# Twelve heads of the first attention batch scored inside the last convolution outputs, and one projection moved a batch later

## The reference, cut to what matters

```
h = silu(conv(x @ w_in_x)) * D * silu(x @ w_in_gate);  x = layernorm(x + h @ w_out)      # (8, 256, 512)
q = x @ Wq.T;  k, v = split(ctx @ Wkv_expand.T)                                          # 16 heads of 32
scores = where(causal, q @ k.T / sqrt(32), lowest);  attn = softmax(scores)
x = layernorm(x + (attn @ v) @ Wout.T)
x = layernorm(x + mixture_of_experts(x))
```

## Time and profile before

| What | us |
|---|---|
| median of 3 runs | 1043.26 |
| lowest and highest of them | 1036.83 and 1044.63 |
| the profiled execution | 1038.53 |
| its span, first to last instruction | 1036.7 |
| PE busy | 973.8 (94%) |
| DVE busy | 678.1 (65%) |
| ACT busy | 528.8 (51%) |
| POOL busy | 257.5 (25%) |

### The profile page before, as it was taken

The page is one execution under the profiler, slowest core; times in us unless marked ns, Lnnn a source line. Parts: engine busy times, 40 slices in busy tenths (PEclk is TensorE's granted clock), DMA queues, the critical chain, the costliest instruction groups (busy, mean ns, idle before and its releaser), DMA issues. The chain is left out here.

```text
span 1036.7 us, 17387 instructions
## 1 busy us (share of the span) xinstructions
PE 973.8 (94%) x5776; PEld 830.6 (80%) x5776; DVE 678.1 (65%) x1554; ACT 528.8 (51%) x1264; POOL 257.5 (25%) x373
## 2 busy tenths in 40 slices
PE   7899999999978999998889979999999999999996
PEld 6688888888867888887667769989888988778785
DVE  4737636378358788887567656777777775254576
ACT  5533414325358889889753146656656664221120
POOL 4610020102133333333530022222222220503040
PEclk9999999999996999998899999999999999999999
DMA  4503005021695989997540268778877882615041
GB/s 163 203 1 122 0 14 199 0 82 61 199 207 140 277 226 260 249 246 192 204 153 21 94 213 282 246 235 279 275 252 249 265 270 78 226 39 202 1 171 73
DMA packets 87758, 172.74 MB, mean 167 GB/s; under 512 B 8624, under 2 KB 36528, under 8 KB 85904
## 3 DMA queue, kind: packets, MB, share of 16 engines
q1 hardware_dynamic: 80560, 149.95, 46.5%
q0 software_dynamic: 7136, 22.03, 6.5%
HBM read 131.05 MB, written 37.49 MB: 163 GB/s over the span
## 5 line engine op out<-in xcount | busy, mean ns | idle before, releaser
L45 PE MATMUL a_ps_proj<-region_a_rounded,arena 128*128 128x512 f32 x272 | 107.8, 396 | 10.3 <-DVE region_a_rounded L369 6.2
L805 ACT ACTIVATE b_dump<-b_dump,b_peak 128x128 f32<-128x128 f32 (+1 forms) x256 | 113.2, 446 | 6.1 <-DVE b_peak L939 5.8
L45 PE MATMUL e_ps_h<-e_x_lo,e_gu_hi 128*128 128x256 f32 (+1 forms) x384 | 110.5, 288 | 2.6 <-DVE e_x_lo L2160 1.3
L47 PE MATMUL e_ps_h<-e_x_hi,e_gu_hi 128*128 128x256 f32 (+1 forms) x384 | 107.6, 280 | 0.0
L46 PE MATMUL e_ps_h<-e_x_hi,e_gu_lo 128*128 128x256 f32 (+1 forms) x384 | 107.5, 280 | 0.0
L46 PE MATMUL a_ps_proj<-region_a_rounded,arena 128*128 128x512 f32 x272 | 106.8, 393 | 0.0
L47 PE MATMUL a_ps_proj<-region_a_rounded,arena 128*128 128x512 f32 x272 | 106.8, 393 | 0.0
L388 DVE SCALAR_TENSOR_TENSOR f_region_b<-a_ps_proj,a_taps,f_region_b 128x510 f32<-128x510 f32 (+2 forms) x96 | 71.7, 746 | 40.8 <-ACT f_region_b L328 38.5
L939 DVE CUSTOM_DVE_ANT_0 b_dump<-b_ps_s,b_mask 128x128 f32<-128x128 f32 (+1 forms) x256 | 80.1, 352 | 22.4 <-PE b_ps_s L1140 19.4
L2166 DVE TENSOR_TENSOR e_gu_lo<-f_region_a,e_gu_hi 128x704 fp32r<-128x704 f32 x92 | 81.3, 887 | 14.9 <-ACT e_gu_hi L2072 14.2
L2072 ACT ACTIVATE e_gu_hi<-f_region_a 128x704 fp32r<-128x704 f32 x92 | 71.8, 784 | 23.1 <-PEq L1476 15.2
(11 more groups left out here) (407 smaller groups left out, 2662.1 us busy)
## 6 DMA issues: line engine op xcount, KB each, us to landing
f_region_a<-we_gate_up SPq DMA_DIRECT2D x88, 352.0 KB, 4.9
qk_split<-arena SPq DMA_DIRECT2D x24, 512.0 KB, 6.2
y_slots<-f_region_b SPq DMA_DIRECT2D x16, 512.0 KB, 4.0
f_x_next<-x SPq DMA_DIRECT2D x6, 1024.0 KB, 7.5
b_sk<-qk_split SPq DMA_DIRECT2D x24, 256.0 KB, 4.4
b_sq<-qk_split SPq DMA_DIRECT2D x24, 256.0 KB, 6.1
f_region_a<-we_down SPq DMA_DIRECT2D x12, 512.0 KB, 4.5
f_region_b<-we_down SPq DMA_DIRECT2D x11, 512.0 KB, 4.1
```

Of the source, the lines that this page charges most:

```text
L45: pe.matmul(out, a_hi, b_lo, start=first, stop=False)
L47: return pe.matmul(out, a_hi, b_hi, start=False, stop=last)
L805: ins = act.activation(dump[:, n % DUMPS, cols], dump[:, n % DUMPS, cols], ACT.Exp, scale=-1.0, bias=peak[:, u, k, i:i + 1], accum_out=tot ...
```

## The change

Four things, in one diff. First, the scores, maxima and totals of heads 0 to 11 of batch 0 move into the convolution's last group: after each `three_pass` of j = 5, 6 and 7 stands one head's score, in the two banks that the projections have left; `maxima` and `totals` of these heads follow on DVE and ACT, and DVE's four residual additions are set between the last four maxima. The logarithm and the subtraction for heads 0 to 7 are done there too. Second, the DMAs of that stretch are issued from three queues: SP keeps 8 key stacks, 4 query stacks and the 4 stores of queries; POOL gets 4 key stacks, the 4 stores of keys, a memset of the two rows of ones and 4 query stacks; ACT gets 4 query stacks. Third, the prologue works heads 12 to 15 alone. POOL there issues three of batch 1's stack loads ahead of `load_peaks`. ACT's table load and POOL's mask move into the convolution's block. Fourth, batch 2 is projected in t = 0, by the same hand order as in the later batches. The buffers of the softmax become a class `Softmax`, alive over both blocks; `dump` of the convolution lies over `hf`.

```diff
+DUMPS = 3
+EARLY = 12
...
-            store_ahead(0, k_hi)
-            store_ahead(1, k_lo)
-            for r, tile in enumerate((k_hi, k_lo, k_hi)):
-                stack_ahead(sp, first_sk, r, tile)
+            stack_ahead(sp, first_sk, 0, k_hi, first_stacked)
+            stack_ahead(sp, first_sk, 2, k_hi, first_stacked)
             sp.wait_ge(ahead_lo_done, 1 + 3 * DC)
             sp.wait_ge(ahead_ready, 3 * DC)
+            stack_ahead(sp, first_sq, 0, q_lo, first_stacked)
             store_ahead(2, q_hi)
             store_ahead(3, q_lo)
-            for r, tile in enumerate((q_lo, q_hi, q_hi)):
-                stack_ahead(sp, first_sq, r, tile)
-            sp.wait_ge(ahead_stored, 16 * (6 * HC + 8))
+            sp.wait_ge(ahead_stored, 16 * 4)
+            sp.wait_ge(first_stacked, 16 * 4 * HC)
...
+            pool.wait_ge(ahead_lo_done, 1 + 2 * DC)
+            pool.wait_ge(h_done, JC * GROUPS)
+            pool.wait_ge(w_lo_done, ALL_UNITS)
+            stack_ahead(pool, first_sk, 1, k_lo, pool_moved)
+            for kind, tile in enumerate((k_hi, k_lo)):
+                for u in range(2):
+                    pool.dma_start(split_dram[1, u, kind].rearrange("p (c t) -> p c t", c=DC // 2).bitcast(F32),
+                                   tile[:, 2 * u:2 * u + 2, S:2 * S].bitcast(F32)).then_inc(pool_moved, 16)
+            pool.memset(rounded[1][K_ROWS:M_ROWS].bitcast(F32), 1.0)
+            pool.wait_ge(ahead_hi_done, 1 + 3 * DC)
+            pool.wait_ge(ahead_ready, 3 * DC)
+            stack_ahead(pool, first_sq, 1, q_hi, pool_moved)
+            pool.wait_ge(pool_moved, 16 * (2 * HC + 4))
...
+            act.wait_ge(ahead_hi_done, 1 + 3 * DC)
+            act.wait_ge(ahead_ready, 3 * DC)
+            stack_ahead(act, first_sq, 2, q_hi, first_stacked)
+            act.preload_act_table_set("natural_log_exp_and_others")
+            for n in range(EARLY):
+                act.wait_ge(max_done, n + 1)
+                soft.add_up(act, dump, n).then_inc(total_done, 1)
+                if n == UH - 1:
+                    act.wait_ge(total_done, UH)
+                    soft.log(act, 0).then_inc(log_done, 1)
...
-            add_x(GROUPS - 1, x1)
+            dve.wait_ge(consts, 3)
+            for n in range(EARLY):
+                maxima(n)
+                if n >= EARLY - TILES:
+                    add_x(LAST, x1, [n - (EARLY - TILES)])
+                if n == EARLY - 2:
+                    dve.wait_ge(log_done, 1)
+                    soft.lower(dve, 0).then_inc(soft.shift_done, 1)
...
+            def score(n):
+                if n == 0:
+                    pe.wait_ge(ahead_lo_done, 1 + 3 * DC)
+                    pe.wait_ge(first_stacked, 16 * 4 * HC)
+                    pe.wait_ge(pool_moved, 16 * (2 * HC + 4))
+                if n >= 2:
+                    pe.wait_ge(max_done, n - 1)
+                q, k = (r[0:K_ROWS, n * S:(n + 1) * S] for r in rounded)
+                soft.score(pe, ps_proj[:, 1, n % 2], q, k).then_inc(s_ready, 1)
...
                         if j == JC - 1:
                             mm.then_inc(out_done, 1)
+                        if j >= scored:
+                            score((j - scored) * TILES + t)
...
-            output(LAST, BEFORE, JC)
+            output(LAST, BEFORE, JC, JC - EARLY // TILES)
...
         def projected(t):
-            return {-1: GB, 0: B}.get(t, t + 2)
+            return t + 2
...
-            for u in range(2):
-                load_stack(1, u)
-            for t in range(FIRST_T, END_T):
+            stack(sp, sk, 1, 0, (KH, KL, KH), stack_loaded[0])
+            load_stack(1, 1)
+            for t in range(END_T):
...
+            stack(pool, sq, 1, 0, (QL, QH, QH), pool_moved)
+            load_peaks(0, 0)
             context(GB)
...
-            for k in sk:
-                pool.memset(k[K_ROWS:M_ROWS].bitcast(F32), 1.0).then_inc(consts, 1)
-            pool.wait_ge(consts, 7)
-            load_peaks(0, 0)
+            pool.memset(sk[1][K_ROWS:M_ROWS].bitcast(F32), 1.0).then_inc(consts, 1)
...
-            act.preload_act_table_set("natural_log_exp_and_others")
...
+            totals(0, 1, EARLY - UH)
+            peaks(0, 0)
+            totals(0, 1, EARLY - UH + 1)
             context(GB)
-            totals(0, 0, 2)
             turned(GB, 0)
             turned(GB, 1)
-            for i in range(3, UH):
-                totals(0, 0, i)
...
+            for i in range(EARLY - UH + 2, UH):
                 totals(0, 1, i)
             logs(0, 1)
...
+            values(0, 1)
+            maxima(0, 1, EARLY - UH)
+            peaks(0, 0)
+            values(0, 0)
+            for i in range(EARLY - UH + 1, UH):
+                maxima(0, 1, i)
+                if i == UH - 2:
                     turned(GB, 0)
                     turned(GB, 1)
...
+                    if b == 1 and u == 0:
+                        pe.wait_ge(pool_moved, 16 * (2 * HC + 4 + 3))
...
+            peaks(0, 0)
+            value(0, 1)
+            scores(0, 1, EARLY - UH)
+            value(0, 0)
+            for i in range(EARLY - UH + 1, UH):
                 scores(0, 1, i)
+            turn(GB, 0)
+            turn(GB, 1)
```

More of the change, by code:

```diff
@@ L91, in moments_step, with __init__, score, least @@
         dve.tensor_tensor(ln.var[:], ln.sq_eps[:], ln.diff_sq[:], ALU.add).then_inc(var_done, 1)
+HEADS = 16
+HD = D // HEADS
+HC = P // HD
+L = 128
+SCALE = 1.0 / float(HD) ** 0.5
+MASKED = -1e30
+UH = HEADS // 2
+BT = S // P
+K_ROWS = 3 * HD
+M_ROWS = K_ROWS + 2
+DUMPS = 3
+EARLY = 12
+class Softmax:
+    def __init__(self, sb, sem):
+        self.mask = sb("mask", [P, 3 * P])
+        self.peak = sb("peak", [P, 2, BT, UH])
+        self.total = sb("total", [P, 2, BT, UH])
+        self.log_total = sb("log_total", [P, 2, BT, UH])
+        self.shift = sb("shift", [P, 2, BT, UH])
+        self.consts = sem("consts")
+        self.pool_moved = sem("pool_moved")
+        self.s_ready = sem("s_ready")
+        self.max_done = sem("max_done")
+        self.total_done = sem("total_done")
+        self.log_done = sem("log_done")
+        self.shift_done = sem("shift_done")
+    def score(self, pe, bank, q, k):
+        for r in range(BT):
+            mm = pe.matmul(bank[:, r * P:(1 + 2 * r) * P], q[:, r * P:(r + 1) * P], k[:, 0:(r + 1) * P], start=True, stop=True)
+        return mm
+    def least(self, dve, dump, bank, n):
+        h = n % HEADS
+        for k, cols in ((0, slice(0, P)), (1, slice(P, 3 * P))):
+            ins = dve.tensor_tensor_reduce(dump[:, n % DUMPS, cols], bank[:, cols], self.mask[:, cols],
+                                           -SCALE, 3e38, ALU.add, ALU.min, self.peak[:, h // UH, k, h % UH:h % UH + 1])
+        return ins
+    def add_up(self, act, dump, n):
+        h = n % HEADS
+        for k, cols in ((0, slice(0, P)), (1, slice(P, 3 * P))):
+            piece = dump[:, n % DUMPS, cols]
+            ins = act.activation(piece, piece, ACT.Exp, scale=-1.0, bias=self.peak[:, h // UH, k, h % UH:h % UH + 1],
+                                 accum_out=self.total[:, h // UH, k, h % UH:h % UH + 1])
+        return ins
+    def log(self, act, u):
+        return act.activation(self.log_total[:, u], self.total[:, u], ACT.Ln)
+    def lower(self, dve, u):
+        return dve.tensor_tensor(self.shift[:, u], self.peak[:, u], self.log_total[:, u], ALU.subtract)
@@ L273, in _ @@
             pool.memset(ln.power[:], -0.5).then_inc(ln_const, 1)
+            pool.memset(soft.mask[:], 0.0).then_inc(consts, 1)
+            pool.wait_ge(consts, 1)
+            for c in (0, 2):
+                pool.affine_select(out=soft.mask[:, c * P:(c + 1) * P], in_=soft.mask[:, c * P:(c + 1) * P],
+                                   compare_op=ALU.is_ge, fill=MASKED, base=0, pattern=[[-1, P]], channel_multiplier=1)\
+                    .then_inc(consts, 1)
             def split_w(u):
@@ L1138, in scores @@
                 q, k = (s[b % 2][0:K_ROWS, u, i] for s in (sq, sk))
-                for r in range(BT):
-                    mm = pe.matmul(ps_s[:, n % 2, r * P:(1 + 2 * r) * P], q[:, r * P:(r + 1) * P], k[:, 0:(r + 1) * P],
-                                   start=True, stop=True)
-                mm.then_inc(s_ready, 1)
+                soft.score(pe, ps_s[:, n % 2], q, k).then_inc(s_ready, 1)
             def peaks(b, u):
```

157 lines of the change are left out of this document (50 added, 107 removed).

## The result

The changed kernel took 1044.22 us (median of 18 runs, 1040.59 to 1047.02), the kernel before, on the same chip, 1038.65 us (18 runs): a ratio of 1.0051, 95% interval 1.0039 to 1.0063. It is 5.6 us slower, where 1038 had been forecast with a gain of 3.1. The profiled execution after took 1046.52 us, its span is 1044.9.

The account below looks back on a forecast made before the run. PE was taken to bound the convolution's last output, ACT t = 0, with PE, ACT and DVE all near their limit in t = 1. 7.1 us gained less 4.0 gave 3.1 faster; from 1040.9, forecast 1038, range 1028 to 1048.

Parts of the forecast that it names:

- First term: Convolution's end: PE waits 3.1 us for the stack moves, first score at 288.0, bounds 284.9 and 291.1.
- Second term: Convolution's end, twelve score slots and tail: 7.3 us to score 8, then 5.7; block starts at 301.3, 7.7 us later.
- the rival of late stacks: Convolution's end: score 0 at 291.1, PE stands 6 us, half-clock slots cost 3 more; 3 us slower, 1044; chance 0.17.
- Third term: Short prologue: its longest chain takes 10.3 us, bounds 9.3 and 12; first exponent at 311.6, 7.1 us gained.
- It doesn't do what it says: Prologue rival: peak rows queue behind POOL's loads, landing 15 us into the block; exponent about 317, 1043; chance 0.06.
- Fourth term: Batch t = 0 with the projection: 28.2 us, 4.0 more, DVE 24.5 busy; ends 1.0 and 7.4 more.
- The sum: Seam and t = 0 together: 7.1 gained less 4.0 is 3.1 us faster; best 10 faster, worst 5 slower.

Follow-up runs that it names:

- 3: Changed kernel with eight instead of twelve heads early in the convolution's end: 1039.11 us, ratio 1.0009.
- 12: Kernel of 1 with 11 products nobody reads ahead of score 0 and 24 in t = 0: 1041.81 us, ratio 1.0026.
- 1: Changed kernel with all of batch 1's stack loads on SP, the second half issued only behind the peak rows: 1040.05 us, ratio 1.0007.
- 4: Changed kernel with 20 products nobody reads on PE behind the turning of batch 2's input, ahead of t = 0: 1046.94 us, ratio 1.0082.
- 7: Changed kernel with POOL's three stack loads given back to SP, which issues all twelve at once; POOL's queue carries only the peak rows: 1042.81 us, ratio 1.0041.
- 10: Kernel of 9 with more products nobody reads, 12 behind the last early score and 13 in the prologue: 1039.13 us, ratio 1.0001.
- 5: Changed kernel with the edits of 1 and 3 together: 1038.57 us, ratio 0.9999.
- 9: Kernel of 5 with 24 products nobody reads in t = 0: 1037.91 us, ratio 1.0000.
- 14: Kernel of 9 run again unchanged, for a second profile: 1038.86 us, ratio 0.9994.

## Why the prediction was wrong, step by step

**First term: right, with some luck in the number.** Score 0 was forecast at 288.0 with a wait of 3.1 us, and came at 287.82 after 2.77. Three queues did not add up. From 270 to 288 the DMA engines moved 262 GB/s at a share of 0.96; in the same 18 us of the kernel before it was 247 at 0.90 (before, then after):

```profile
270.00:288.00 18.00, 18.00 (x81) 14.81 (x80) 2.08 (x3) 1.79 (x3) 0.00 (x0) 1.00 0.90 247
...
270.00:288.00 18.00, 15.23 (x69) 12.26 (x67) 2.08 (x3) 3.08 (x4) 10.09 (x12) 1.00 0.96 262
```

The forecast's 4.2 MB in 18.1 us are 232 GB/s. The rate was higher, but some 0.5 MB of SP's query stores moved among the stacks, which the forecast had left to its upper bound; the two offset each other. What three queues issued sooner landed later (the first line is the kernel before, the others are the kernel after):

```profile
region_b_rounded<-arena SPq DMA_DIRECT2D x12, 128.0 KB, 2.6
...
region_b_rounded<-arena SPq DMA_DIRECT2D x8, 128.0 KB, 5.5
...
region_a_rounded<-arena ACTq DMA_DIRECT2D x4, 128.0 KB, 5.3
region_a_rounded<-arena POOLq DMA_DIRECT2D x4, 128.0 KB, 4.3
```

These are moves of that stretch with their median microseconds from issue to landing. The Trainium skill (DMA: Bandwidth & Descriptors, "Issuing engines are not separate DMA queues") says that issuing from several engines saves only the time to issue. The trace agrees, but for 6% more bytes in that time. The prediction took this rule for a wait of 3.1 us and, in the rival of late stacks, for one of 6; it holds no rate, so both rest on the rows alone.

**Second term: the size was off by 1.6 us.** The slots were priced at full clock directly behind a wait that I had forecast myself; the fall of the clock stood only in the rival of late stacks, tied to a wait of 6 us. 2.77 us were enough: the first two slots took 1.77 and 1.71 us, the later ones 0.93, and score 8 came 9.05 us behind score 0 instead of 7.3; the tail was 6.0, as forecast. Without the wait (3) or with the wait filled (12) the loss was gone, and 12 met the term's 301.3. The size of the loss varied: in 1 and 4 four slots were slow, and the block started 2.8 us later than in 12, counted from score 0.

**Third term: the step that failed by most.** "its 0.79 MB need 7.6 us, so the peak rows land some 9 us into the block, just in time": they were usable 13.5 us into it. The step had given POOL's queue half of all bandwidth and counted the rows as done with the loads. POOL's three loads did land by 9.6 us into the block; the rows, issued at 4.4 us into it, were usable 9.1 us after that, behind SP's loads as well as POOL's (7). This is what the rival "It doesn't do what it says" describes, and it had the exponent at about 317 (317.12 measured) with a chance of 0.06. The chain itself was good: where the rows do not hold it, 11.0 to 11.3 us (12 and 1) against 10.3, inside its bounds. Of the 3.9 us that the prologue took beyond the term, 3.1 are ACT's wait in front of the first exponent.

**Fourth term: taken near the wrong bound.** 28.2 us were forecast with DVE as the limit and PE's low clock hidden in "its slack of 7.7 us"; it took 31.39, at the upper end of 31.6. DVE was busy for 22.75, not over 24, and waited for PE. The slack did not hide the clock: ACT waited 8.3 us and DVE 6.5 for PE over the batch, and in 331 to 335, at a clock of 0.84, they were busy for 2.49 and 2.67 of 4 us. At a clock of 1.00 the batch takes 26.81 (10), with DVE busy for 23.14 and idle for 3.67. So the term's 3.7 of DVE idle came out there, by luck: the prediction gave no row for it, and its rows say 5.3 and 4.5. Two smaller slips: ACT's idle of 1.6 is in no row (0.64 in t = 0, 2.79 in t = 1), and 4 us at 0.61 cost 1.6 us, not 1.7. Neither changes the result. Of the 3.2 us in excess, 2.6 went when the rows came early (1); why that changes t = 0 so much I can't separate from where the clock's falls lie.

**The sum.** 1.6 + 3.9 + 3.2 + 0.5 (t = 1, which I had equal to before) = 9.2 us, from 3.1 ahead to 6.0 behind at t = 2. By these terms the change would have been worth the forecast only with the clock held and the rows in time; no kernel measured here shows it. No mix of its parts came out below the kernel before by more than the noise: the best, experiments 5, 9 and 14, equal it within some 0.3%. The prediction's remark that a change under 1% can't be told from none was too cautious: with 18 runs of each the interval is 0.24% wide.

Open: why the filled kernels, up to 3 us ahead at t = 2, are not faster. A wait for the residual explains 2 us in 10 and 14 and is counted at t = 2 already. The rest, 667 to 674 us behind t = 2, differed between executions of one kernel (9 and 14). But from the start of t = 2 to the last product of the router's block the four edits of the changed kernel with fillers in t = 0 (9, 10, 12, 14) took 2.1 to 6.4 us longer than before, all other runs at most 2.5. That hints at a cost of the fillers themselves; with one profile of each I can't tell it from a draw.

## What to carry to other kernels

When idle engines are given work from a neighbouring stage, price the engine that is left alone there: here a wait of 2.8 us cost another 1.6 us in slots at half clock, and a stage's "slack" at full clock was no cover. Put the smallest transfer that ends a chain ahead of the bulk loads of all queues, not behind them; behind them, 2 rows delayed a batch by 3 us. Ask of each added queue how full the DMA engines already are: from a share of 0.90 there were 6% of rate to win, besides an earlier issue.

## What the runs showed of the hardware that was not expected

ACT's four DMA issues held it from 276.79 to its table load at 282.68, with nothing else to wait for in the trace: 1.47 us each, where I had taken 0.72. POOL's four in the same stretch took 2.21 us, 0.55 each. SP's last four stack issues took 4.96 us, 1.24 each, against 0.72 before. So with three queues in use SP's issues were slower than before and ACT's slower than I had taken, POOL's were not; why is not shown. SP's last one ended at 284.3, not at the 280.4 forecast, and score 0 waited for that move; whether it would have landed earlier for an earlier issue, on engines busy at 0.96, is open too.
